# Two-layer MLP with per-row experts: the second stage taken row by row, with 512- and 256-column products and two sums per tile

## What is computed

```python
h = gelu(einsum('bnd,hd->bnh', x, fc1_w) + fc1_b)        # 1024 hidden features
shared = einsum('bnh,sh->bns', h, fc2_w) + fc2_b         # 192 outputs
expert_x = einsum('bnh,bph->bnp', h, experts_w[indices]) + experts_b[indices][:, None, :]   # 64 outputs
return x + concatenate([shared, expert_x], axis=-1)
```

## Time and profile before

| | |
|---|---|
| three runs, us | 363.24, 363.62, 364.08 (median 363.62) |
| profiled execution, us | 363.34 |
| its span (first to last instruction), us | 361.5 |
| PE busy | 356.4 us, 99% of the span |
| PE weight loads | 350.3 us, 97% |
| DVE, ACT, POOL busy | 62%, 67%, 61% |
| granted TensorE clock, mean | 0.998 |

### The profile page before, as it was taken

How to read it: one execution, slowest core, us unless ns; L and a number is a source line. 1 busy time by engine, 2 the same in 40 slices (tenths; PEclk the granted TensorE clock), 3 DMA queues, 4 the chain that set the end, 5 groups by cost and what they waited for, 6 DMA issues and landing times.

```text
span 361.5 us, 7842 instructions
## 1 busy us (share of the span) xinstructions
PE 356.4 (99%) x2863; PEld 350.3 (97%) x2863; DVE 224.0 (62%) x367; ACT 243.6 (67%) x410; POOL 222.2 (61%) x100
## 2 busy tenths in 40 slices
PE   8999999999999999999999999999999999999996
PEld 6898999999999999999999999999999999999996
DVE  1797993937758285683937658395673938653241
ACT  3794865757849576694857759576794857757560
POOL 0079824676655677565676655677565577655381
PEclk9999999999999999999999999999999999999999
DMA  8869856361703426044261603526052321403011
GB/s 202 183 160 117 156 143 150 126 160 45 175 22 116 127 69 173 31 124 89 82 160 52 168 25 109 132 82 162 29 140 74 94 91 58 126 18 100 2 58 58
DMA packets 70447, 37.86 MB, mean 105 GB/s; under 512 B 43530, under 2 KB 70410, under 8 KB 70410
## 3 DMA queue, kind: packets, MB, share of 16 engines
q1 hardware_dynamic: 69792, 36.85, 40.8%
q10 hardware_dynamic: 618, 0.53, 0.6%
HBM read 28.97 MB, written 8.39 MB: 103 GB/s over the span
## 4 chain that ended last, share of the span: by engine, by line
PE 95%; issue 2%; POOL 1%; ACT 1%; DVE 0%; POOLq 0%
PE fc_ps L985 37%; PE acc_ps L1017 16%; PE acc_ps L1021 16%; PE acc_ps L1019 16%; PE fc_ps L961 6%; PE fc_ps L930 1%; POOL ht L353 1%; PE tr_ps L924 1%; PE fc_ps L968 1%; ACT ht L510 0%; ACT gelu L536 0%; DVE work L794 0%; DVE resid L819 0%; ACT w1t L430 0%; PE acc_ps L924 0%
## 5 line engine op out<-in xcount | busy, mean ns | idle before, releaser
L353 POOL TENSOR_TENSOR ht<-gelu,ht 128x1024 fp32r<-128x1024 f32 x60 | 144.5, 2408 | 121.3 <-ACT ht L510 121.3
L985 PE MATMUL fc_ps<-xt,w1t 128*128 128x256 f32 x1176 | 173.2, 283 | 0.0
L985 PEld LDWEIGHTS fc_ps<-xt,w1t 128*128 128x128 f32 x1176 | 155.3, 192 | 0.1
L1017 PE MATMUL acc_ps<-w2t,ht 128*128 128x256 f32 x512 | 144.9, 283 | 0.2 <-POOL ht L353 0.2
L1019 PE MATMUL acc_ps<-w2t,ht 128*128 128x256 f32 x512 | 144.9, 283 | 0.0
L1021 PE MATMUL acc_ps<-w2t,ht 128*128 128x256 f32 x512 | 144.9, 283 | 0.0
L1017 PEld LDWEIGHTS acc_ps<-w2t,ht 128*128 128x128 f32 x512 | 98.3, 192 | 0.6 <-POOL ht L353 0.3
L1019 PEld LDWEIGHTS acc_ps<-w2t,ht 128*128 128x128 f32 x512 | 98.3, 192 | 0.3
L1021 PEld LDWEIGHTS acc_ps<-w2t,ht 128*128 128x128 f32 x512 | 98.3, 192 | 0.0
L510 ACT ACTIVATE ht<-gelu 128x1024 fp32r<-128x1024 f32 x64 | 68.0, 1062 | 3.3
L496 ACT ACTIVATE work<-fc_ps 128x512 f32<-128x512 f32 x28 | 16.8, 600 | 57.4 <-PE fc_ps L985 57.4
(11 more groups left out here) (57 smaller groups left out, 279.5 us busy)
## 6 DMA issues: line engine op xcount, KB each, us to landing
pieces<-in_L_cond_experts_w SPq DMA_DIRECT2D x128, 64.0 KB, 2.0
out<-resid SPq DMA_DIRECT2D x32, 256.0 KB, 3.0
pieces<-in_x SPq DMA_DIRECT2D x60, 128.0 KB, 3.6
resid<-in_x SPq DMA_DIRECT2D x15, 512.0 KB, 4.1
bias<-in_L_cond_experts_b SPq DMA_DIRECT2D x32, 32.0 KB, 2.9
w_piece<-in_L_cond_fc_w SPq DMA_DIRECT2D x4, 256.0 KB, 4.5
w_piece<-in_L_cond_fc_w SPq DMA_DIRECT2D x4, 192.0 KB, 5.0
resid<-in_x SPq DMA_DIRECT2D x2, 256.0 KB, 3.4
```

Of the source, the lines that this page charges most:

```text
L353: nc.gpsimd.tensor_tensor(ht[:, slot, LO, :, :].rearrange("p k t -> p (k t)"), gelu[:, q % GELUS, :, :].rearrange("p k t -> p (k t)"), ht[ ...
L985: last = nc.tensor.matmul(fc1_ps[:, dst, j * SEQ:(j + 1) * SEQ], w1t[:, w, wv, ms], xt[:, n % 2, o, xv, :], start=(fresh and j == 0 and at ...
L1017: nc.tensor.matmul(dst, h_hi_t, w_hi, start=(r == 0 and u % (2 * T) == 0), stop=True, skip_group_check=True)
```

## The change

The second stage goes by row of the batch. `fc2(i, ...)` is one pair of one row: four units (two chunks by two tiles). In a unit the high part of h streams the high and the low columns of w2 in one product of 512, into the two halves of a bank, and the low part of h streams the high columns in one of 256, into the second half. So a bank belongs to a tile and holds two sums, and both rows use the same two banks in turn: the first units of a row wait, tile by tile, for the drain of the row before. The pairs of h are read twice, once by each row, and stay longer: `ht` gets six slots. A drain adds both sums of each tile: 8 additions for row 0 (192 and 64 columns), 4 for row 1 (256), where the second sum of a tile waits for the first. The bias is split in two tiles and two instructions a row. In the opening, 24 units stand where 32 stood; 40 stand behind the last group. Expert weights are squared and split by row, not by half of the chunks. The orders of all engines are written anew. On PE a group t runs, with i = 6 + 4t: `product4(t-1)`, the four units of fc2(i), product 1, the four of fc2(i+1), products 2, 5 and 6, three units of fc2(i+2), product 3, its last unit and one of fc2(i+3), product 7, and the last three units of fc2(i+3).

```diff
+    SLOTS = 6
...
-        ht = sbuf("ht", [P, PAIRS, 2, 2, TOK], FP32R)
+        ht = sbuf("ht", [P, SLOTS, 2, 2, TOK], FP32R)
...
         def _(sp):
             numbers = load_experts(0)
+            load_expert_bias(0, numbers)
+            sp.dma_start(bias[:, :], fc2_b.rearrange("(o n) -> o n", o=1).to_broadcast([P, SHARED]))\
+                .then_inc(b2_loaded, 16)
             load_x_pieces(1)
-            load_expert_bias(0, numbers)
             load_x_pieces(2)
             numbers = load_experts(1)
             load_w1_pieces()
-            sp.dma_start(
-                bias[:, :, :, 0:SHARED].rearrange("p a b o -> p (a b) o"),
-                fc2_b.rearrange("(o c n) -> o c n", o=1, c=1).to_broadcast([P, 2 * R, SHARED]))\
-                .then_inc(b2_loaded, 16)
...
         def _(pool):
-            def residual(n):
+            def residual(n, b):
...
+                pool.wait_ge(b2_loaded, 16)
                 pool.wait_ge(be_loaded[par], 16 * R * (n // 2 + 1))
...
+            residual(0, 0)
             for r in range(PAIRS):
                 pair_lo(r)
             x_sums_lo(PLAIN)
...
         def _(act):
...
             def pair_high(q):
-                if q >= PAIRS:
-                    act.wait_ge(fc2_pair, q - PAIRS + 1)
+                if q >= SLOTS:
+                    n, r = divmod(q - SLOTS, PAIRS)
+                    act.wait_ge(fc2_done, fc2_end(n, R - 1, r))
...
             for n in range(PLAIN, BLOCKS):
                 for g in range(GROUPS):
                     t = group(n, g)
-                    if g == 0:
+                    if g == 1:
                         experts_high(n - 1, 1)
+                    elif n + 1 <= LAST:
+                        b_copy(n + 1)
+                        x_high(n + 1)
                     if t > 0:
                         upper_pair(t - 1)
                     s1_copy(t)
-                    if g == 0 and n + 1 <= LAST:
-                        b_copy(n + 1)
-                        x_high(n + 1)
+                    if g == 1:
+                        experts_high(n, 0)
                     s5_copy(t)
...
         def _(dve):
             def drain(n, b):
+                dve.wait_ge(resid_ready, 4 * n + 2 * b + 2)
+                for t in range(T):
+                    if t == 0:
+                        dve.wait_ge(tile_filled, R * n + b + 1)
+                    else:
+                        dve.wait_ge(fc2_done, fc2_end(n, b, PAIRS - 1))
+                    dst = resid[:, n % 2, b * T + t, :]
+                    for v in (HI, LO):
+                        src = acc_ps[:, t, v * OUT:(v + 1) * OUT]
+                        if v == LO:
+                            dve.wait_ge(drained, drained_at(n, b, t) - additions(b))
+                        if b == 0:
+                            nc.vector.tensor_tensor(dst[:, 0:SHARED], src[:, PART:OUT],
+                                                    dst[:, 0:SHARED], ALU.add)\
+                                .then_inc(drained, 1)
+                            nc.vector.tensor_tensor(dst[:, SHARED:OUT], src[:, 0:PART],
+                                                    dst[:, SHARED:OUT], ALU.add)\
+                                .then_inc(drained, 1)
+                        else:
+                            nc.vector.tensor_tensor(dst, src, dst, ALU.add).then_inc(drained, 1)
...
             experts_square(1, 0)
+            drain(0, 0)
             plain_low(4)
             s_square(0)
             experts_low(1, 0)
...
             s_square(2)
-            experts_square(1, 1)
             s_low(2)
-            drain(0, 0)
-            drain(0, 1)
             plain_low(6)
+            dve.wait_ge(s_lo, 4)
+            for d in range(D):
+                x_square(PLAIN + 1, d)
             plain_low(7)
 
             for n in range(PLAIN, BLOCKS):
                 for g in range(GROUPS):
                     t = group(n, g)
...
                     if g == 0 and n + 1 <= LAST:
                         x_sums_first(n + 1)
                         x_low(n + 1, 0)
                         x_sums_last(n + 1)
+                    if g == 1:
+                        experts_low(n - 1, 1)
...
+                        experts_square(n, 0)
+                    if g == 0:
+                        drain(n - 2, 1)
+                    else:
+                        drain(n - 1, 0)
+                    add_c11(t)
                     add_v(t)
...
                     add_c12(t)
                     if g == 0:
...
+                        experts_square(n - 1, 1)
+                        add_c22(t)
                     else:
...
+                            x_square(n + 2, 0)
+                        add_c22(t)
+                        if n + 2 <= LAST:
+                            x_square(n + 2, 1)
...
         def _(pe):
+            def fc2(i, first, count):
+                n, b, r = i // (R * PAIRS), i // PAIRS % R, i % PAIRS
                 q = PAIRS * n + r
                 for u in range(first, first + count):
+                    j, t = u // T, u % T
                     k = chunk_of(q, j)
                     if u == 0:
                         wait_h_lo(pe, q)
...
+                    if r == 0 and j == 0 and i > 0:
+                        pe.wait_ge(drained, drained_at(n - (1 - b), 1 - b, t))
+                    ts = slice((b * T + t) * P, (b * T + t + 1) * P)
+                    nc.tensor.matmul(acc_ps[:, t, :].rearrange("p (v o) -> p v o", v=2),
+                                     ht[:, q % SLOTS, HI, j, ts], w2t[:, :, k, fc2_columns(b)],
+                                     start=(k == 0), stop=True, skip_group_check=True)
+                    last = nc.tensor.matmul(acc_ps[:, t, OUT:2 * OUT],
+                                            ht[:, q % SLOTS, LO, j, ts],
+                                            w2t[:, HI, k, fc2_columns(b)],
+                                            start=False, stop=True, skip_group_check=True)
+                    if u == 3:
+                        last.then_inc(fc2_done, 1)
+                    elif r == PAIRS - 1 and u == 2:
+                        last.then_inc(tile_filled, 1)
...
-            fc2_units(0, 0, 0, 8)
+            fc2(0, 0, 4)
+            fc2(1, 0, 4)
             pe.wait_ge(x1_lo, D)
             conv_chunk(K)
-            for at in range(6):
-                fc2_units(0, 1 + at // 2, at % 2 * 4, 4)
-                conv_chunk(K + 1 + at)
+            conv_chunk(K + 1)
+            for at in range(4):
+                fc2(2 + at, 0, 4)
+                conv_chunk(K + 2 + at)
+            conv_chunk(2 * K - 2)
             conv_chunk(2 * K - 1)
...
             product4(LAST_T)
-            fc2_units(LAST, 0, 2, 6)
-            for r in range(1, PAIRS):
-                fc2_units(LAST, r, 0, 8)
+            for i in range(6 + 4 * (LAST_T + 1), R * PAIRS * BLOCKS):
+                fc2(i, 0, 4)
```

More of the change, by code:

```diff
@@ L88, in cond_mlp_residual @@
         pieces = sbuf("pieces", [P, 4, M * XJ])
-        bias = sbuf("bias", [P, 2, R, OUT])
+        bias = sbuf("bias", [P, SHARED])
+        e_bias = sbuf("e_bias", [P, 2, R, PART])
         ident = sbuf("ident", [P, P])
@@ L272, in store @@
             def store(n, b):
-                sp.wait_ge(drained, drained_at(n, b))
+                sp.wait_ge(drained, drained_at(n, b, T - 1))
                 ts = slice(b * T, (b + 1) * T)
@@ L306, in _ @@
             load_x_pieces(3)
-            sp.wait_ge(e_sq, 2)
+            sp.wait_ge(e_sq, R)
             numbers = load_experts(2)
-            sp.wait_ge(resid_ready, 1)
+            sp.wait_ge(x_sq, 2 * D)
+            load_x_pieces(4)
+            sp.wait_ge(resid_ready, 4)
             load_expert_bias(2, numbers)
-            for n in range(1, BLOCKS):
-                if n >= 2:
-                    store(n - 2, 1)
+            store(0, 0)
+            for n in range(PLAIN, BLOCKS):
                 if n + 3 <= LAST:
@@ L336, in _ @@
         def _(pool):
-            def residual(n):
+            def residual(n, b):
                 par = n % 2
                 if n == 0:
-                    for b in range(R):
-                        pool.wait_ge(x0_loaded[b], 16)
+                    pool.wait_ge(x0_loaded[b], 16)
+                    pool.wait_ge(x0_tr, D)
                 else:
                     pool.wait_ge(x_loaded[par], 16 * ((n + 1) // 2))
+                pool.wait_ge(b2_loaded, 16)
                 pool.wait_ge(be_loaded[par], 16 * R * (n // 2 + 1))
-                rows = resid[:, par, :, :].rearrange("p (b t) d -> p b t d", b=R)
+                rows = resid[:, par, b * T:(b + 1) * T, :]
                 nc.gpsimd.tensor_tensor(
-                    rows, rows, bias[:, par, :, :].unsqueeze(2).to_broadcast([P, R, T, OUT]),
+                    rows[:, :, 0:SHARED], rows[:, :, 0:SHARED],
+                    bias[:, :].unsqueeze(1).to_broadcast([P, T, SHARED]),
+                    ALU.add).then_inc(resid_ready, 1)
```

(54 more changed lines are left out.)

179 lines of the change are left out of this document (79 added, 100 removed).

## The result

| | before | after |
|---|---|---|
| runs beside each other, us | 363.24 to 364.08, median 363.82 | 369.44 to 371.05, median 369.87 |
| ratio, 95% interval | | 1.0174 (1.0147 to 1.0200) |
| again, beside the experiments, us | 363.66 | 369.48 |
| ratio, 95% interval | | 1.0152 (1.0139 to 1.0165) |
| profiled execution, its span, us | 363.34, 361.5 | 369.44, 367.4 |

A forecast was written before the change was run, and what follows sets the result against it. PE's sum of products was taken as the bound, each PE wait adding in full: -5.1 + 3.2 + 0.85 + 0.2 + 3.65 + 3.45 = +6.25 on 363.34 us gives 369.6 us, range 364.0 to 375.0.

The forecast's parts named there:

- 512 units: Second stage: a unit costs 0.350 us instead of 0.360, one product start saved; -5.1 us (4.1 to 6.1 saved).
- (a): Opening: POOL's low parts wait behind the bias, and row 0 uses pairs up faster; +3.2 us (1.7 to 10.7).
- (b): Opening, pair 3: PE arrives before POOL's low part is ready; +0.85 us (0.7 to 1.0).
- (c): Between rows 0 and 1 of block 0: PE waits for tile 1 to be drained; +0.2 us.
- (d): Block 0: `drain(0,0)` holds DVE's list, so `drain(0,1)` is late and fc2(8) waits; +3.65 us (1.5 to 5.5).
- the end: Behind the last group: waits for drains at two row changes, 1.28 and 1.56, last drain 0.60; +3.45 us (2.8 to 4).
- Rivals 1 and 3: Units: 1, cheaper pairs, 361.9 us, chance 0.12; 3, a product's fixed part only as bf16 shows, 373.4 us, chance 0.03.
- rival 4: Waits at (a) and (d) also lower the clock, adding some 3 to 4 us: 373 to 374 us; chance 0.06.
- Steady groups: The 28 groups between opening and end: drains and additions come in time; taken as nothing, 0 to 0.8 us.

The follow-up runs named there:

- e4_two_256: Changed kernel with each 512-column product split into two of 256 columns, 512 more products in all: 372.31 us, +2.8 beside the changed kernel.
- e5_bias_later: Changed kernel with POOL's bias additions for row 0 of block 0 moved behind the low parts of pairs 0 to 2: 367.21 us, ratio 1.0122 to before.
- e1_no_low: Changed kernel without DVE's four subtractions that make the low parts of block 1's h: 365.83 us, -3.7 beside the changed kernel.
- e8_order: Changed kernel with DVE's and ACT's instructions reordered around groups 0 and 1, drains, additions and copies going earlier: 367.13 us, ratio 1.0094 to before.
- e2_clock: Changed kernel with 7 dummy bf16 products ahead of product 6 of group 0 and 12 behind it, keeping PE busy: 368.09 us, -1.7 beside the changed kernel.
- e3_end_banks: Changed kernel with both rows of block 15 put into PSUM banks already free by then: 366.30 us, -3.6 beside the changed kernel.

## Why the prediction was right

It said 369.6 us; the runs gave 369.87. By its own steps, against the two profiles of the changed kernel (delays are counted in starts of products; where there are two figures, the first profile's stands first):

| step | predicted, us | measured, us |
|---|---|---|
| 512 units | -5.1 | -4.5 |
| (a) bias in front, and the pace of row 0 | +3.2 | +1.3 and +2.2 |
| (b) pair 3 | +0.85 | +0.25 |
| (c) between rows 0 and 1 of block 0 | +0.2 | +0.2 |
| (d) fc2(8) behind DVE's list | +3.65 | +4.3: waits 3.2 and 2.8, clock 1.1 and 1.5 |
| the end | +3.45 | +3.55 |

- **The unit.** 0.0088 us, not 0.010, in the range; e4_two_256 shows it by itself. Rivals 1 and 3, by which it would have been worth 12.8 or 1.3 us, are out.
- **(a)** The mechanism holds (e5_bias_later: 1.1 us in the trace), the size was too large. The bias was issued at 14.03 us, not 14.5, and landed 4.1 us later, not 4.5, and the latency from POOL's end to PE is 0.05 us (19.74 + 4.75 = 24.49, the unit at 24.54), not 0.47: in the earlier trace rows PE had not been waiting when the unit started at 21.04; it arrived then. The same misread price made (b) too large. In the second profile the first unit is 1.28 us later than the 21.04 of before and fc2(1) another 0.96; in the first it is 1.16 later, but 0.8 of that lies in front of the first plain product and is no part of the change. With the 0.8 the steps of the first profile add to 5.9 us, those of the second to 6.0, where the profiled executions differ by 6.1 and 6.2.
- **(d)** DVE reached `drain(0,1)` at F + 17.36 (predicted 17.78) and fc2(8) started at F + 18.38 (18.79), with F = 33.33, the start of the chunk behind fc2(3). The wait was smaller than I worked out, and PE spent part of it earlier: product 6 waited for ACT's copy, which stands behind copies of x that wait for the same list of DVE. I had not seen that wait, 0.99 and 0.56 us in starts. e1_no_low and e8_order show that the list, not the drain, is the cause.
- **The clock** was rival 4, and my sum put it at nothing. The rival was right at one of its two places, (d): 1.1 and 1.5 us, of the 3 to 4 that it priced for both; e2_clock gives 1.5 back in its trace and 1.7 us in time. In the opening, (a), the clock stayed at 1.00, and behind fc2(8) it did not fall in every profile (e4_two_256, e5_bias_later). That the sum came out within 0.3 us is luck in part: the clock fills much of what (a), (b) and the wait of (d) fell short.
- **The end.** In starts, row 14/1 to 15/0 costs 0.94 + 0.34 = 1.28 and row 15/0 to 15/1 1.07 + 0.48 = 1.55, where I had 1.28 and 1.56; the last drain ends 1.72 us after the start of the last product, not 1.00: 0.72 for 0.60. e3_end_banks shows that the waits are for banks; the last drain, (b) and (c) were taken out by no run of their own.
- **Steady groups:** nothing, as taken.

## What to carry to other kernels

When PE is the bound and a rewrite saves a little in every step, look for the few places where the pattern is not steady (first and last blocks, a change of banks): here 4.5 us saved in 512 units were outweighed by some ten waits, and with the orders around those places rewritten much the same units are 0.9% faster than the kernel before. Before you move an instruction, follow it through all engines that wait for it, and look at what the other engines run beside the idle stretch that it is to fill.
